# Two-layer conditioned transformer on one core: attention in unrolled steps of 8 heads in place of 4

## The reference

```python
mod = silu(c) @ w_adaln + b_adaln                     # 6 vectors of 144 a batch
sh_msa, sc_msa, g_msa, sh_mlp, sc_mlp, g_mlp = split(mod, 6)
q, k, v = heads(_modulate(_ln(x), sh_msa, sc_msa) @ w_qkv + b_qkv)
attn = softmax(einsum('bhqd,bhkd->bhqk', q, k) * hd ** -0.5)
x = x + g_msa * (einsum('bhqk,bhkd->bhqd', attn, v) @ w_proj + b_proj)
xf = _modulate(_ln(x), sh_mlp, sc_mlp)
# layer 0
cw = softmax over the top 2 of (xf @ w_gate), 0 for the others
x = x + g_mlp * sum_e cw[e] * (gelu(xf @ w1[e] + b1[e]) @ w2[e] + b2[e])
# layer 1 (separate wq, wk, wv, norms with weights, exact gelu)
x = x + g_mlp * (gelu(xf @ fc1_w + fc1_b) @ fc2_w + fc2_b)
```

## Time and profile before

| | us |
|---|---|
| median of 3 runs (607.68 to 619.57) | 608.32 |
| the profiled execution | 610.86 |
| its span, first to last instruction | 609.1 |
| PE, DVE, ACT, POOL busy in it | 504.9, 338.6, 263.0, 116.1 |

### The profile page before, as it was taken

One profiled execution on the slowest core, in us unless ns is written; L12 is line 12 of the kernel. 1 busy time (PEld: TensorE's weight loads), 2 busy tenths in 40 slices (PEclk: granted clock), 3 DMA queues, 4 the chain that ended last, 5 costly groups with the idle time before them and its releaser, 6 DMA issues.

```text
span 609.1 us, 11960 instructions
## 1 busy us (share of the span) xinstructions
PE 504.9 (83%) x4098; PEld 386.4 (63%) x4098; DVE 338.6 (56%) x1002; ACT 263.0 (43%) x549; POOL 116.1 (19%) x122
## 2 busy tenths in 40 slices
PE   5726997878867899999999999658787986998886
PEld 5414665556545567997988979645654654665765
DVE  8635436566767654361542625467466776654662
ACT  1313413545546446426145173136264553555441
POOL 9020200100203900603206024202010020000000
PEclk9955855797987579999999999959689787989999
DMA  5044382252452500000000000443324245110111
GB/s 177 2 104 144 84 190 76 67 134 64 109 144 76 137 18 2 2 19 1 2 19 0 8 12 6 117 128 86 112 67 123 80 103 137 62 27 1 40 39 58
DMA packets 50893, 42.33 MB, mean 69 GB/s; under 512 B 33089, under 2 KB 43256, under 8 KB 50846
## 3 DMA queue, kind: packets, MB, share of 16 engines
q1 hardware_dynamic: 49762, 41.51, 25.3%
q10 hardware_dynamic: 1088, 0.26, 0.2%
HBM read 33.20 MB, written 8.29 MB: 68 GB/s over the span
## 4 chain that ended last, share of the span: by engine, by line
PE 37%; issue 37%; DVE 8%; DMA 7%; ACT 4%; POOL 4%; SPq 1%; DVEq 0%; POOLq 0%; ACTq 0%
PE bank L1392 13%; PE bank L1193 4%; DMA QA<-mT 4%; PE bank L1196 3%; PE bank L1194 3%; PE bank L1195 3%; POOL parts L619 3%; DMA KA<-qk_scratch 2%; PE bank L1188 2%; DMA qk_scratch<-parts 2%; PE bank L1406 1%; DVE mp L1003 1%; PE bank L1249 1%; PE bank L1227 1%; POOL rstd L612 1%
## 5 line engine op out<-in xcount | busy, mean ns | idle before, releaser
L747 ACT ACTIVATE pr<-bank 128x512 f32<-128x512 f32 x128 | 76.7, 599 | 98.7 <-PE bank L1238 95.4
L995 DVE TENSOR_REDUCE mx<-bank 128x4 f32<-128x512 f32 x128 | 86.2, 685 | 51.8 <-PE bank L1227 48.8
L1227 PE MATMUL bank<-KA,QA 81*128 81x128 bf16 x512 | 60.7, 255 | 31.2 <-DMA KA<-qk_scratch 27.7
L1392 PE MATMUL bank<-w_sb,hid 128*128 128x144 f32 x640 | 81.1, 286 | 0.0
L1392 PEld LDWEIGHTS bank<-w_sb,hid 128*128 128x128 f32 x640 | 79.8, 190 | 0.6
L1238 PE MATMUL bank<-QA,KA 83*128 83x128 bf16 x512 | 58.9, 247 | 20.2 <-DMA QA<-mT 19.7
L1227 PEld LDWEIGHTS bank<-KA,QA 81*128 81x128 bf16 x512 | 42.1, 115 | 49.2 <-DMA KA<-qk_scratch 19.9
L1249 PE MATMUL bank<-pr,V 128*32 128x128 f32 x1024 | 62.9, 324 | 3.0 <-ACT pr L747 3.0
L612 POOL TENSOR_TENSOR rstd<-var_eps,minus_half 128x4 f32<-128x4 f32 x16 | 16.2, 1011 | 256.8 <-DVE var_eps L945 256.8
L830 ACT ACTIVATE hid<-bank 128x512 f32<-128x512 f32 x72 | 41.2, 601 | 50.7 <-PE bank L1196 50.6
L1238 PEld LDWEIGHTS bank<-QA,KA 83*128 83x128 bf16 x512 | 40.9, 112 | 25.5 <-issue 12.9
(11 more groups left out here) (188 smaller groups left out, 942.0 us busy)
## 6 DMA issues: line engine op xcount, KB each, us to landing
QA<-qk_scratch SPq DMA_DIRECT2D x32, 324.0 KB
KA<-qk_scratch SPq DMA_DIRECT2D x96, 108.0 KB
qk_scratch<-parts SPq DMA_DIRECT2D x16, 384.0 KB, 3.2
...
```

What stands on the lines that cost most here:

```text
L747: sc.activation(pr[:, q % 2, :], bank[ST_BANK[q % 2]][:, :], ACT.Exp, scale=SCALE).then_inc(s["exp_s"], 1)
L995: v.tensor_reduce(mx[:, HQ * q:HQ * (q + 1)], bank[S_BANK[q % 2]][:, :].rearrange("p (h k) -> p h k", k=SEQ), AX.X, ALU.max).then_inc(s["m ...
L1227: last = te.matmul(bank[S_BANK[q % 2]][:, i * SEQ:(i + 1) * SEQ], QA[0:SROWS, j, h, :], KA[0:SROWS, j, h, :], start=True, stop=True)
L1392: last = te.matmul(dst, hid[:, at:at + SEQ], w2_sb[:, MT1 * e + i, :], start=(i == 0), stop=(i == MT1 - 1))
```

## The change

A step becomes eight heads: `PAIRS = 2` steps a batch, 32 a layer. The scores of a MAX go into one pair of banks (s_pair), those of a SCORE into another (st_pair), and one reduction and one exp read 1024 columns. There is one pair of each, so MAX waits for the maximum of the step before (`max_s`), SCORE for the exp of the step before (`exp_s`). MAX runs four steps ahead; MAX_T is two steps ahead of the batch's first SCORE, and its store is issued by SP.

The preparation of the group that starts at step 8i lies at fixed distances r before it: statistics -23, moments -22, normalisation -20 and -16, transposes -15 and -14, split -13, QK -12 to -10, parts -11 to -9, stores -10 to -8, values -9 and -8, loads -7, -5, -3, -1. The scratch has a place of its own for each group, V has two halves. The loops are gone: all groups are written out, and all waits are on constants. The modulation is two rows of 432 columns a layer (ACT copies them, PE transposes four of the six vectors from there); the rows of -1 come by a DMA; h's rest part is modulated on ACT; the late weights of layer 0 are loaded two DMAs a step, rounded and split in ten pieces over steps 14 to 25; V has 10 columns a head in place of 32. In the feed-forward part the normalisation is two groups ahead (after the DOWNs), the transposes are inside UP, and layer 1's first QK stands after DOWN 0, 1 and 2.

```diff
-QUADS = 4
-HQ = HEADS // QUADS
-AHEAD = 5
-LEAD = 6
+PAIRS = 2
+HP = HEADS // PAIRS
+LEAD = 4
...
+        s_pair = ctx.enter_context(nc.psum_tensor("s_pair", [P, 1024], F32))
+        st_pair = ctx.enter_context(nc.psum_tensor("st_pair", [P, 1024], F32))
...
+        def prep_order(L, p):
...
+            for i in range(1, G + 2):
+                n, a = n0 + i, a0 + i
+                if i < NG:
+                    r = p - GP * i
+                    if r in (-20, -16):
+                        first.append(("APPLY", (n, (0, 1) if r == -20 else (2, 3))))
+                    if r == -23:
+                        first.append(("STATS", n))
+                    if r == -22:
+                        first.append(("MOMENTS", n))
+                    if -10 <= r <= -8:
+                        first.append(("STORE", (a, r + 10)))
+                    if -11 <= r <= -9:
+                        first.append(("PART_R", (a, r + 11)))
+                        mid.append(("PART_B", (a, r + 11)))
+                    if r == -15:
+                        late.append(("H_MAIN", n))
...
+                    if -12 <= r <= -10:
+                        late.append(("QK", (a, r + 12, False)))
+                    if r in (-9, -8):
+                        late.append(("V", (a, r + 9, False)))
+                    if -7 <= r <= -1 and r % 2:
+                        late.append(("LOAD", G * a + (r + 7) // 2))
...
+        def attention_order(L):
+
+            B0, P0 = BATCH * L, NP * L
+            for p in range(-LEAD, NP + 3):
+                b, h = p // PAIRS, p % PAIRS
+                first, mid, late = prep_order(L, p)
+                if p + LEAD < NP:
+                    yield "MAX", P0 + p + LEAD
+                if h == 0 and 0 <= b + 1 < BATCH:
+                    yield "MAX_T", B0 + b + 1
+                yield from first
+                if 0 <= p < NP:
+                    yield "SCORE", P0 + p
+                yield from mid
+                if h == 0 and 0 <= b - 2:
+                    yield "PROJ", B0 + b - 2
+                if h == 1 and 0 <= b - 1 < BATCH:
+                    yield "OUT_T", B0 + b - 1
...
+                yield from late
+                if 0 <= p - 1 < NP:
+                    yield "PV", P0 + p - 1
+                if h == 1 and 0 <= b - 1 < BATCH:
+                    yield "ATT_T", B0 + b - 1
...
-                with eng.Fori(1, NG - 1) as g:
-                    group(attention_order(False, False), attention, L, g)
...
+        def program():
+
+            for L in range(2):
+                yield from prologue(L)
+                yield from attention_order(L)
+                for g in range(NG):
+                    yield from mlp_order(L, g)
...
+            def store_max(B):
+
+                sp.wait_ge(s["mt_c"], B + 1)
+                sp.dma_start(QA[SROWS:MROWS, B % G, :, :], mT[:, :]).then_inc(s["m_ld"], 16)
...
-            def m_store(B, j):
-
-                need(act, "mt_c", B + 1)
-                act.dma_start(QA[SROWS:MROWS, j, :, :], mT[:, :]).then_inc(s["m_ld"], 16)
-
-            def exp_quad(qi, q):
-                need(act, "st_mm", qi + 1)
-                need(act, "pv_mm", qi - 1)
-                sc.activation(pr[:, q % 2, :], bank[ST_BANK[q % 2]][:, :], ACT.Exp,
-                              scale=SCALE).then_inc(s["exp_s"], 1)
+            def exp_pair(Pn):
+                act.wait_ge(s["st_mm"], Pn + 1)
+                need(act, "pv_mm", Pn - 1)
+                sc.activation(pr[:, Pn % 2, :], st_pair[:, :], ACT.Exp, scale=SCALE).then_inc(s["exp_s"], 1)
...
+                v.tensor_reduce(mx[:, HP * h:HP * (h + 1)], s_pair[:, :].rearrange("p (h k) -> p h k", k=SEQ),
+                                AX.X, ALU.max).then_inc(s["max_s"], 1)
...
-            def scores(a, B, j, q):
-
-                qi = 4 * B + q
-                need(pe, "max_s", qi - 1)
+            def scores(Pn):
+
+                B, h = Pn // PAIRS, Pn % PAIRS
+                a, j = B // G, B % G
+                need(pe, "max_s", Pn)
...
-                need(pe, "exp_s", 4 * B + q - 1)
+                need(pe, "exp_s", Pn)
...
```

1274 lines of the change are left out of this document (618 added, 656 removed).

## The result

The changed kernel takes 575.95 us (median of 4 runs, 575.46 to 581.87), the kernel before beside it 613.03: a ratio of 0.9495, 95% interval 0.939 to 0.96. It is faster, as forecast, but by 37 us where 93 were predicted (515 us), and above the range (486 to 568). The profiled run took 576.06 us, its span 574.0.

The account below looks back on a forecast made before the run. PE bounds feed-forward 0; in the attentions no engine is full, and PE waits and drops clock. 55.5 + 117.8 + 165.5 + 9 + 114.7 + 53 = 515.5 us of span, 517.3 with 1.8 around it, corrected to 515; range 486 to 568.

Parts of the forecast that it names:

- The steady unit: Attention, 8 heads: 4.55 us less 0.9 of waits and 0.15 gives 3.5; with clock, 3.8 (layer 0) and 3.7 us.
- C: Rival for the attention units: slower, the single buffer keeps PE at the low clock; 661 us, chance 4%.
- A: Rival for the attentions: SP's queue delays the maxima's stores and holds the scores up; 563 us, chance 17%.
- B: Rival for the attention units: all stalls go and the clock stays up, 3.15 us a unit; 478 us, chance 10%.
- D: Rival for the attention units: no gain, a unit costs as much as before; 582 us in all, chance 4%.
- First score at 55.5: Start to first score of layer 0: 55.5 us for 57.15, from QK starting 1.6 us earlier.
- the way into layer 1: Between feed-forward 0 and attention 1: 9 us in place of 17.3, bounds 7 and 14.
- Attention 0, 31 times 3.8: Layer 0's attention, last to first score: 31 units of 3.8 us, 117.8 us, a gain of 50.
- The clock term: Added to each attention unit: a quarter of what half clock cost before, 0.34 us in layer 0, 0.18 in layer 1.
- Feed-forward 0, 165.5: Layer 0's feed-forward: same matmuls with PE full, 165.5 us for 165.80.
- The rest, 53: Behind attention 1, with feed-forward 1: 53 us for 60.6, 2.5 us gained in three groups; bounds 51 and 60.

Follow-up runs that it names:

- p2: Changed kernel with MAX of units 1 and 3 put in the second pair of banks ahead of the first score; 570.45 us, ratio 0.9269.
- p1: Changed kernel with VectorE's subtraction for group 1's product put ahead of the row maxima in the four steps before the first score; 563.31 us, ratio 0.9179.
- p3: Changed kernel with group 1's three products in three banks instead of one, in both layers; 566.14 us, ratio 0.9231.
- p8: Changed kernel with the edits of p1 and p3, and that of p4 in layer 1 only; 563.56 us, measured again 568.38 us.
- p7: Changed kernel with the late weight loads started at unit 6, three a unit, instead of unit 0, two a unit; 572.28 us, ratio 0.9337.
- p10: p8 with the late weight loads started four units ahead of the first score instead of at it; 565.18 us, ratio 0.9206.
- p16: p8 with p12's and p14's edits, and the 1.2 MB late load moved behind the read of group 1's second batch; 555.65 us, ratio 0.8990.
- p9: Changed kernel with GpSimd's eighteen subtractions for the weights' low parts cut to 4 columns each; 571.83 us, ratio 0.9339.
- p14: p8 with eight (layer 1: five) instead of four UPs in attention's last steps, put ahead of the waiting instructions; 559.97 us, ratio 0.9104.
- p4: Changed kernel with VectorE's split of the next group's inputs put behind the first DOWN's residual in both feed-forwards; 574.26 us, ratio 0.9355.
- p12: p8 with the eighteen subtractions for the weights' low parts done by VectorE instead of GpSimd; 558.96 us, ratio 0.9063.

## Why the prediction was wrong, point by point

- *The steady unit* came out in the number: attention 1 115.85 us for 114.7, its units 8 to 19 3.55 us each at full clock for 3.5, maxima 1224 ns for 1215, exp 1027 for 1029. The working was in part luck. I took 0.9 us of waits off a unit, 59.8 us over 64; but 59.8 us are the waits of the whole span, only 37.6 of them lie in the two attentions, and in the stretch that gave the 4.55 us the same three rows have 3.7 us, 0.5 a unit. In the other direction waits for `an` and `resid` of 14.7 and 12.6 us (before: 2.7 and 2.2) stand in the changed attentions 0 and 1. What made the unit that much shorter all the same is not shown.
- *Rivals*: C (the single buffer keeps the clock low) is out, since the clock was 0.88 and 0.81, units 8 to 19 ran at 1.00, and p2 moved nothing. A is out by the missing row, B by the unit (3.7 and 4.2 us for 3.15), D by the unit too (4.38 and 5.25), though its 582 us for the whole is the nearest of all: near by accident, as the units gained what the stages around them lost.
- *"First score at 55.5" and "the way into layer 1", 9 us* are the terms that failed most clearly, +10.2 and +13.1 us. I took over the old distance from first MAX to first SCORE in layer 0 (10.5 us; it became 20.9), and in layer 1 counted two MAX and their maxima, a transpose and a store. In fact five MAX stand ahead of the first SCORE, with a product of the next group between each two, through one bank and one VectorE queue: 4.87 us a step. The QK did start 1.6 us earlier, as predicted, and the first MAX 1.5 us earlier, but the ring behind it took 10.4 more. p1 and p3 gave back 4 to 5 us in each; p8's 15.7 and 13.7 are still above the prediction. In these TensorE works 10.8 and 10.5 us: the products, which before stood behind the first SCORE, now stand ahead of it, and I had put none of them there.
- *Attention 0, 31 times 3.8*: +13.7. I priced only the unit. The loads (units 0 to 7: p7, p10, p16) cost 4.5 to 6.4 us in their units and the splitting of the weights (units 20 to 25: p9) 6.3, but taking one away did not shorten the stage by as much. p9's whole stage was 127.1, p14's 126.9; no run reached 117.8.
- *The clock term* was mis-sized in both: I left a quarter of the time at the lower clock, 22 and 11 us, and put 10.5 and 5.6 us into the sum for it. Measured were clocks of 0.81 and 0.88 where above 0.9 was forecast, which is 50 and 28 us at the lower clock. By the prediction's own rule (half of it) that would be 25 and 14 us, an estimate from these clocks, and an upper one: units 20 to 25 of attention 0 did not follow the clock.
- *Feed-forward 0, 165.5*: +10.8. I had moved nothing into it. Of this 7.5 us lie between last score and first DOWN. There TensorE's idle time grew from 0.7 to 3.7 us, the last batch draining in whole steps of 8 heads with nothing between its waits; the other 4.5 us are busy: p8's first profile, at a clock of 1.00, works 24.6 us there for 21.7 before (141 matmul records for 111), so some 2.9 us are work that the new order has put there, such as the next group's transposes, and some 1.6 the lower clock. p14 had 25.80 in place of 29.84. The other 3 lie in the groups behind: first DOWN to last 146.1 us after, 143.2 before, with 3.4 us idle against 1.6; which edit does it was not tried.
- *The rest, 53*: +9.5. The drain is 6.3 us longer (15.4 for 9.1), and the groups behind it gained 4.1 us (47.1 for 51.2) of the 7.6 forecast; the residual behind the split is 1.6 us of what is missing (p4). The step that failed is the same: an early split and UPs were taken as pure gain, without what is queued behind them.

What stays open: why a stall removed in one part of attention 0 so often comes with a lower clock in another (p7, p9, p10, p16: units 8 to 19 at 0.85 to 0.93 instead of 1.00). In p7, p10 and p16 the waits for KA that moved there are a part of it, but smaller than the loss. p9 has none, and p2, p12 and p8 again took 48.7, 47.6 and 47.5 us there at clocks of 0.93 to 0.96 with nothing edited in these units but p12's split; so it is not shown that one brings the other.
